# A six-stage transformer kernel: the scan's layer norm partly on ScalarE, one feed-forward norm inside the scan, three other seams reordered

## The reference

```python
x = x + _L0_xattn_ref(_layernorm(x), ctx_1024, ctx_1024, mask, ...)   # 16 heads, masked
x = x + _L0_attn_ref(_layernorm(x), L0_attn_context, ...)             # 8 heads of 128, shared context
x = x + _L0_ffn_ref(_layernorm(x), ...)                               # six attention nodes ("cell")
x = x + _L1_xattn_ref(_layernorm(x), ctx_1024)                        # no weights
x = x + _L1_attn_ref(_layernorm(x), ...)                              # linear scan over the sequence
x = x + _L1_ffn_ref(_layernorm(x), ...)                               # 256 -> 1024 -> 256, gelu
```

## Time and profile before

| | us |
|---|---|
| three runs | 2956.18, 2957.56, 2959.49 (median 2957.56) |
| profiled execution, its own time | 2957.78 |
| span of that execution, first to last instruction | 2955.8 |
| PE busy | 2823.1 (96%) |
| DVE busy | 2156.6 (73%) |
| ACT busy | 2036.0 (69%) |
| POOL busy | 1177.1 (40%) |

### The profile page before, as it was taken

How to read it: one execution, slowest core, us unless ns; L and a number is a source line. 1 busy time by engine, 2 the same in 40 slices (tenths; PEclk the granted TensorE clock), 3 DMA queues, 4 the chain that set the end, 5 groups by cost and what they waited for, 6 DMA issues and landing times. The chain is left out here.

```text
span 2955.8 us, 84436 instructions
## 1 busy us (share of the span) xinstructions
PE 2823.1 (96%) x31996; PEld 2198.5 (74%) x31996; DVE 2156.6 (73%) x5328; ACT 2036.0 (69%) x4128; POOL 1177.1 (40%) x962
## 2 busy tenths in 40 slices
PE   7999999799999999999989999999999999889999
PEld 6888888556666666666677887887888788556798
DVE  7888888777777767777736787787777777678443
ACT  6888888787777777777706766776667777333444
POOL 6777777576665656666600011011011100121310
PEclk9999999999999999999999999999999999999999
DMA  4111111077777887787851112111111103450000
GB/s 152 52 60 50 62 50 50 9 139 147 154 160 155 166 161 163 162 174 154 194 193 63 38 45 73 38 42 46 52 45 46 48 31 137 161 191 1 8 22 29
DMA packets 613611, 275.10 MB, mean 93 GB/s; under 512 B 548763, under 2 KB 589654, under 8 KB 613094
## 3 DMA queue, kind: packets, MB, share of 16 engines
q1 hardware_dynamic: 597958, 231.16, 32.6%
q10 hardware_dynamic: 15360, 39.85, 3.8%
HBM read 119.40 MB, written 17.30 MB: 46 GB/s over the span
## 5 line engine op out<-in xcount | busy, mean ns | idle before, releaser
L1645 POOL TENSOR_TENSOR front_parts<-front_prob,front_parts 128x1024 f16<-128x1024 f32 x256 | 545.6, 2132 | 328.0 <-ACT front_parts L1853 294.4
L1943 DVE TENSOR_REDUCE wide_row_max<-wide_score 128x1 f32<-128x1024 f32 x256 | 312.5, 1221 | 125.9 <-PE wide_score L1686 125.5
L1841 ACT ACTIVATE front_prob<-wide_score,wide_neg_max,front_s_up 128x1024 f32<-128x1024 f32 x256 | 307.7, 1202 | 123.8 <-DVE wide_neg_max L1946 118.7
L1686 PE MATMUL wide_score<-wide_kT,wide_qT 128*128 128x512 f16 x1536 | 375.6, 381 | 6.2 <-ACT front_prob L1841 4.6
L2248 POOL TENSOR_TENSOR cell_w<-cell_w_stage,cell_w 128x1536 fp32r<-128x1536 f32 x23 | 80.5, 3498 | 637.4 <-ACT cell_w L2519 637.4
L954 POOL TENSOR_TENSOR common_common<-common_common,mask_inv_sum 128x512 f32<-128x512 f32 x256 | 272.1, 1063 | 107.8 <-DVE mask_inv_sum L1352 105.2
L1209 ACT ACTIVATE common_common<-common_common,mask_row_min 128x256 f32<-128x256 f32 x512 | 254.8, 502 | 48.0 <-DVE mask_row_min L1300 47.7
L1853 ACT ACTIVATE front_parts<-front_prob 128x1024 f16<-128x1024 f32 x256 | 269.9, 1054 | 13.8 <-ACT front_prob L1841 7.0
L1686 PEld LDWEIGHTS wide_score<-wide_kT,wide_qT 128*128 128x128 f16 x1536 | 144.5, 98 | 154.2 <-ACT front_prob L1841 6.9
L2708 DVE TENSOR_REDUCE cell_row_max<-cell_score 128x8 f32<-128x512 f32 x192 | 131.0, 682 | 152.8 <-PE cell_score L2349 151.0
L1300 DVE CUSTOM_DVE_ANT_0 common_common<-mask_score,front_prob 128x256 f32<-128x256 f32 x512 | 189.1, 417 | 3.5 <-issue 3.5
(11 more groups left out here) (349 smaller groups left out, 6591.6 us busy)
## 6 DMA issues: line engine op xcount, KB each, us to landing
cell_w_stage<-cell_weights ACTq DMA_DIRECT2D x24, 768.0 KB, 5.1
front_cT<-in_ctx_turned SPq DMA_DIRECT2D x32, 512.0 KB, 3.3
ahead_home<-in_ctx_odd SPq DMA_DIRECT2D x16, 1024.0 KB, 5.6
cell_w_stage<-in_L_ffn_W_own ACTq DMA_DIRECT2D x24, 512.0 KB, 3.6
front_prob<-in_mask_BxS_ik SPq DMA_DIRECT2D x32, 256.0 KB, 3.5
front_probT<-front_parts SPq DMA_TRANSPOSE x512, 2.8
ahead_home<-in_ctx_even SPq DMA_DIRECT2D x16, 512.0 KB, 4.0
common_common<-in_L_ffn_W_pairs SPq DMA_DIRECT2D x10, 512.0 KB, 4.3
```

The lines of the kernel that those rows point to most:

```text
L1645: pool.tensor_tensor(parts[:, s % 2, LO, :], prob[:, s % 2, :], parts[:, s % 2, HI, :], ALU.subtract).then_inc(part_lo, 1)
L1686: mm = pe.matmul(score[:, s % 2, half * 512:(half + 1) * 512], qT[:, u_par, a, s * P:(s + 1) * P], kT[:, par, b, half * 512:(half + 1) * 5 ...
L1841: act.activation(prob[:, s % 2, :], score[:, s % 2, :], ACT.Exp, bias=neg_max[:, s % 2:s % 2 + 1], scale=s_up[:, 0:1], accum_out=row_sum[: ...
L1943: dve.tensor_reduce(row_max[:, one], score[:, s % 2, :], AX.X, ALU.max).then_inc(max_found, 1)
```

## The change

It has five parts.

1. Scan: the apply of blocks 3 to 7 moves from VectorE (the end of step n) to ScalarE, behind `gate_of(n + 2)`. GpSimd computes the shift, with two small instructions for each block.
2. Feed-forward norm of block 0: stats and apply on VectorE in step 6 of the scan, around the straight-through of the second weight; its transposes in step 7, ahead of the second weight's; its copies there too. The two `keep_clock` calls go.
3. The low-rank products, merges and splits of the second weight move from the end of the scan into the first `fc` of the feed-forward, one to each of its eight steps.
4. Masked attention: unit 0's rows are the first DMA. Cell: in the last step block 6's stats and apply come ahead of the low half, its scale and add behind it, with the norms of context units 0 and 1 between them; GpSimd's order follows.
5. Feed-forward: the last block is stored in two halves.

```diff
+    def gpsimd_shift(self, pool, n):
+        at = n - self.first_shift + 1
+        pool.tensor_scalar(self.neg_mean[:, :], self.mean_var[:, :, 0], -1.0, None, ALU.mult).then_inc(self.negated, 1)
+        pool.wait_ge(self.negated, at)
+        pool.wait_ge(self.rstd_ready, n + 1)
+        pool.tensor_tensor(self.shift[:, :], self.neg_mean[:, :], self.rstd[:, :], ALU.mult).then_inc(self.shift_ready, 1)
+
+    def scalar_apply(self, act, n, x):
+
+        act.wait_ge(self.turned, n * DH)
+        act.wait_ge(self.shift_ready, n - self.first_shift + 1)
+        for s in range(SUB):
+            ins = act.activation(self.xn[:, s, :], x[:, s, :], ACT.Identity, bias=self.shift[:, s:s + 1], scale=self.rstd[:, s:s + 1])
+        ins.then_inc(self.xn_ready, 1)
...
+    def tensor_low_rank_late(self, pe, banks, t):
+        out, lhsT, rhs, _ = self.products[self.fc_loras + t]
+        if t == 0:
+            pe.wait_ge(self.prep_copied, len(self.turns))
+        if t >= 2:
+            pe.wait_ge(self.weights_ready, self.fc_loras + t - 1)
+        pe.matmul(banks[t % 2][:, 0:rhs.shape[1]], lhsT, rhs, start=True, stop=True).then_inc(self.lora_ready, 1)
...
@@ masked attention, SP @@
+        load_rows(0, 0)
         sp.dma_start(wT[:, :, :, :], W_turned).then_inc(w_loaded, 16)
...
@@ cell, POOL and DVE @@
+            for X in range(1 if last else 2):
+                last_norm.gpsimd_rstd(pool, i * 2 + X)
             if last:
                 for k in range(2):
                     ahead.gpsimd_rstd(pool, k, k)
-            for X in range(1 if last else 2):
-                last_norm.gpsimd_rstd(pool, i * 2 + X)
...
                 if final and X == 1:
-                    for k in range(2):
-                        ahead.vector_stats(dve, k, k)
-                        ahead.vector_apply(dve, k, k)
+                    finish_stats(i, 0, last)
+                    ahead.vector_stats(dve, 0, 0)
+                    ahead.vector_finish_norm(dve, i * 2)
+                    ahead.vector_apply(dve, 0, 0)
                 for hf in range(DH):
...
                 if final and X == 1:
-                    finish(i, 0, last)
+                    ahead.vector_finish_scale(dve, i * 2)
+                    ahead.vector_finish_add(dve, i * 2, 0)
+                    ahead.vector_stats(dve, 1, 1)
+                    ahead.vector_apply(dve, 1, 1)
...
@@ scan, POOL @@
         for n in range(1, NBLK):
+            if n >= FIRST_SHIFT:
+                pool.wait_ge(norm.xn_ready, n)
             norm.gpsimd_rstd(pool, n)
-        ffn.gpsimd_lo(pool, 0, ffn.loras)
+            if n >= FIRST_SHIFT:
+                norm.gpsimd_shift(pool, n)
+        ffn.norm.gpsimd_rstd(pool, 0)
+        ffn.gpsimd_lo(pool, 0, ffn.fc_loras)
...
@@ scan, PE @@
             if n == 7:
+                ffn.norm.tensor_turn(pe, 0, False)
                 ffn.tensor_turn(pe, ffn_banks, ffn.fc_turns, len(ffn.turns))
...
-        ffn.tensor_low_rank(pe, ffn_banks, ffn.fc_loras, ffn.loras)
...
@@ scan, ACT @@
             if follows(n, 2):
                 copy_hi(n + 2)
                 gate_of(n + 2, False)
+            if follows(n, 3):
+                norm.scalar_apply(act, n + 3, of_block(n + 3))
...
             if n == 7:
+                ffn.scalar_turned_hi(act, turn_banks, 0)
                 ffn.scalar_copy(act, ffn_banks, ffn.fc_turns, len(ffn.turns))
-                ffn.scalar_hi(act, ffn.fc_loras, ffn.loras)
...
@@ scan, DVE @@
             if n == 6:
+                ffn.norm.vector_stats(dve, 0, of_block(0))
                 ffn.vector_straight_through(dve, 1)
+                ffn.norm.vector_apply(dve, 0, of_block(0), False)
+            if n == 7:
+                ffn.vector_turned_lo(dve, turn_banks, 0)
             finish(n)
...
-            if n == 7:
-                ffn.vector_merge(dve, ffn_banks, ffn.fc_loras, ffn.loras)
-            if follows(n, 3):
-                norm.vector_apply(dve, n + 3, of_block(n + 3), True)
...
@@ feed-forward, PE @@
-        keep_clock(pe, const["ident"], out_banks[1], 32)
-        norm.tensor_turn(pe, 0, False)
-        keep_clock(pe, const["ident"], out_banks[1], 24)
...
                 mm.then_inc(fc_ready, 1)
+                if first:
+                    ffn.tensor_low_rank_late(pe, out_banks, t)
 
         def project(n, j, first, last):
+            if first:
+                pe.wait_ge(ffn.weights_ready, ffn.loras)
...
@@ feed-forward, ACT (gelu) and DVE (split_hidden) @@
+                if first:
+                    ffn.scalar_hi(act, ffn.fc_loras + t, ffn.fc_loras + t + 1)
...
             for t in range(FT):
+                if first:
+                    ffn.vector_merge_late(dve, out_banks, t)
                 dve.wait_ge(gelu_done, n * FT + t + 1)
```

More of the change, by code:

```diff
@@ L148, in vector_apply, with add_shift @@
         ins.then_inc(self.xn_ready, 1)
+    def add_shift(self, mem, name, first):
+        self.first_shift = first
+        self.neg_mean = mem.sb(name + "neg_mean", [P, SUB])
+        self.shift = mem.sb(name + "shift", [P, SUB])
+        self.negated = mem.sem(name + "negated")
+        self.shift_ready = mem.sem(name + "shift_ready")
+    def gpsimd_shift(self, pool, n):
[10 more added lines that the diff above has]
+        ins.then_inc(self.xn_ready, 1)
     def tensor_turn(self, pe, n, has_last):
@@ L215, in __init__ @@
         self.inv_scale = mem.sb("inv_scale", [P, 2])
+        self.norm = BlockNorm(mem, const, True, name="ffn_")
+        self.xnT = mem.sb("ffn_xnT", [P, 2, DH, BLK], F32R)
+        self.xn_hi = mem.sem("xn_hi")
         self.w_split = {"fc": mem.sb("ws_fc", [P, 2, DH, F], F32R), "proj": mem.sb("ws_proj", [P, 2, FT, D], F32R)}
@@ L363, in tensor_low_rank, with vector_merge_late, scalar_turned_hi, vector_turned_lo @@
             pe.matmul(bank[:, 0:rhs.shape[1]], lhsT, rhs, start=True, stop=True).then_inc(self.lora_ready, 1)
+    def tensor_low_rank_late(self, pe, banks, t):
[5 more added lines that the diff above has]
+        pe.matmul(banks[t % 2][:, 0:rhs.shape[1]], lhsT, rhs, start=True, stop=True).then_inc(self.lora_ready, 1)
+    def vector_merge_late(self, dve, banks, t):
+        n = self.fc_loras + t
+        out = self.products[n][0]
+        dve.wait_ge(self.lora_ready, n + 1)
+        dve.scalar_tensor_tensor(out, banks[t % 2][:, 0:out.shape[1]], self.LORA, out, ALU.mult, ALU.add).then_inc(self.weights_ready, 1)
+    def scalar_turned_hi(self, act, banks, n):
+        for h in range(DH):
+            act.wait_ge(self.norm.turned, n * DH + h + 1)
+            act.activation(self.xnT[:, self.HI, h, :], banks[h][:, :], ACT.Copy).then_inc(self.xn_hi, 1)
+    def vector_turned_lo(self, dve, banks, n):
+        for h in range(DH):
+            dve.wait_ge(self.xn_hi, n * DH + h + 1)
+            dve.tensor_tensor(self.xnT[:, self.LO, h, :], banks[h][:, :], self.xnT[:, self.HI, h, :].bitcast(F32), ALU.subtract)\
+                .then_inc(self.norm.turn_copied, 1)
     def vector_merge(self, dve, banks, first, end):
@@ L893, in _, with load_rows @@
     def _(sp):
+        def load_rows(u, k):
+            sp.dma_start(x_of(u), x_in[rows(u * P, P), :]).then_inc(x_loaded[k], 16)
+        load_rows(0, 0)
         sp.dma_start(wT[:, :, :, :], W_turned).then_inc(w_loaded, 16)
@@ L900, in load @@
                 sp.wait_ge(in_turned, u - 1)
-            sp.dma_start(x_of(u), x_in[rows(u * P, P), :]).then_inc(x_loaded[k], 16)
+            if not isinstance(u, int) or u > 0:
+                load_rows(u, k)
             if later(u):
@@ L3108, in stage_scan @@
     norm.banks = turn_banks
+    FIRST_SHIFT = 3
+    norm.add_shift(mem, "norm_", FIRST_SHIFT)
+    ffn.norm.banks = turn_banks
     wo, wc, wb, wt, rows2 = front.wo, front.wc, front.wb, front.wt, front.rows2
@@ L3321, in stats_of @@
         def stats_of(n):
+            if n > FIRST_SHIFT:
+                dve.wait_ge(norm.shift_ready, n - FIRST_SHIFT)
             norm.vector_stats(dve, n, of_block(n))
@@ L3427, in add_bias @@
             pool.tensor_tensor(of_block(n), of_block(n), ffn.out_bias[:, :].unsqueeze(1).to_broadcast([P, SUB, D]), ALU.add).then_inc(bias_added, 1)
-        norm.gpsimd_rstd(pool, 0)
+        norm.gpsimd_rstd(pool, 1)
+        ffn.gpsimd_lo(pool, ffn.fc_loras, ffn.loras)
         add_bias(0)
-        with pool.Fori(1, NBLK) as n:
+        add_bias(1)
+        with pool.Fori(2, NBLK) as n:
             norm.gpsimd_rstd(pool, n)
@@ L3444, in fc @@
             if first:
[L3445 removed]
+                pe.wait_ge(ffn.w_lo, ffn.fc_loras)
             for t in range(FT):
@@ L3480, in _ @@
     def _(act):
-        def turned_hi(n):
-            for h in range(DH):
-                act.wait_ge(norm.turned, n * DH + h + 1)
-                act.activation(xnT[:, HI, h, :], turn_banks[h][:, :], ACT.Copy).then_inc(xn_hi, 1)
         def gelu(n, j, first, last):
@@ L3530, in low @@
             return dve.tensor_tensor(dst, src, hi.bitcast(F32), ALU.subtract)
-        def turned_lo(n):
```

(5 more changed lines are left out.)

36 lines of the change are left out of this document (21 added, 15 removed).

## The result

The changed kernel took 2984.48 us (median of 4 runs, 2974.07 to 2992.84), the kernel before 2958.52 beside it (4 runs, 2956.18 to 2961.91). The ratio is 1.0079, 95% interval 1.0061 to 1.0097: slower by 26 us, 17.5 above the top of the predicted range.

A forecast was written before the change was run, and what follows sets the result against it. TensorE, busy 96% of the span, was taken as the bound, with more to win in the seams than in the scan. Terms of -2.4 - 3.7 - 0.9 - 0.4 + 4.0 - 0.8 + 4.4 = +0.2 gave 2958.0 us, range 2949 to 2967.

The forecast's parts named there:

- Start and end of the cell: Kernel's start, unit 0's rows issued first: -2.4 us; cell's end, ScalarE's last copy no longer waiting for VectorE: -3.7.
- clock of the seam: Behind the cell, less TensorE idle time may keep its clock up: -0.9 us, between 0 and -1.8.
- store: Kernel's end, only 256 KB left to store behind the last add: -0.8 us, between 0 and -1.5.
- Gaps of the scan: Scan, TensorE waits for ScalarE's apply behind the gate, four gaps of 3.45 us: +11.1.
- Steps 4 to 7: Late scan, a later ScalarE copy, block 0's stats and apply, and eight transposes lengthen the path: +5.95 us.
- Seam to the feed-forward: Scan's last add to first `fc`, only barrier and start remain, 0.9 us in place of 18.3: -17.4.
- First `fc`: First feed-forward block, eight low-rank products between groups and a late last merge: +4.0 us, bounds 2.5 and 6.
- The clock in the scan: Scan, TensorE's clock may fall in four gaps, 1.1 us each, between 0 and 2.2: +4.4.
- Rival C: Scan, the clock falls at each boundary and stays low: 2964.9 us, 2970 at 4 a gap; chance 0.22.
- Rival B: Scan, the moved apply stays hidden, TensorE's gap remaining near 0.65 us: 2941 us; chance 0.07.

The follow-up runs named there:

- e4: The kernel before with only unit 0's rows first, the cell's last norm reordered and the last store in two halves: 2950.13 us, ratio 0.9966.
- e1: The changed kernel with 32 identity transposes put back ahead of the first `fc`: 2970.78 us, ratio 1.0055.
- e9: The changed kernel with one edit, ScalarE's apply in the scan ahead of the gate instead of behind it: 2948.28 us, ratio 0.9954.
- e8: The changed kernel with the apply ahead of the gate and the low-rank products two each behind `fc` groups 4 to 7: 2938.97 us, ratio 0.9935.
- e7: The changed kernel with the low-rank products two each behind groups 4 to 7 of the first `fc`, scan untouched: 2983.36 us, ratio 1.0075.
- e11: The kernel before with only the apply of blocks 3 to 7 moved to ScalarE, behind the gate: 2995.36 us, ratio 1.0112.
- e10: The changed kernel with 28 identity transposes starting scan steps 1 to 4, and low-rank products behind `fc` groups 4 to 7: 2956.85 us, ratio 0.9991.
- e3: The changed kernel with 32 identity transposes ahead of the first `fc` and ScalarE's apply ahead of the gate: 2942.24 us, ratio 0.9949.
- e12: The kernel before with only the apply of blocks 3 to 7 moved to ScalarE, ahead of the gate: 2955.17 us, ratio 0.9986.
- e2: The changed kernel with the second weight's low-rank products, merges and splits back at the scan's end, no transposes: 2967.64 us, ratio 1.0036.

## Why the prediction was wrong

The sum was made of terms, most of them right.

- Start and end of the cell, -2.4 and -3.7, clock of the seam -0.9, store -0.8: right, and e4 measured -8.9 for all four. The start gave more than its term: the wide attention's first transposes stand at 563.5 on average in the eleven profiles with the new start and at 566.8 in the three without, 3.3 earlier. PE's idle time behind the cell fell from 5.36 to 1.71. The scan starts 6.34 earlier in the profile, but the cell with that idle time took 1031.6 to 1038.2 us among those eleven, so one profile can't weigh this.
- Gaps of the scan, +11.1: right in mechanism and size (13.6 in four waits, less the 2.6 of before).
- Steps 4 to 7, +5.95: it was 7.2, and the clock makes the difference. From the scan's first transposes to the end of its last product PE takes 25.1 us longer (124.4 against 99.3). Of these 1.0 lie ahead of the first gap, where the clock was lower (0.50 in the first 2.7 us, transposes of 1.94 in place of 1.06), and 16.9 in the four steps, 11.0 as gaps and 5.8 as clock. Behind them 7.2 are left. The wait for the small transposes is as forecast: 2.37 in place of 0.41 and 1.06, +0.9 for +0.95. But the clock fell in it as well, and the step behind it is 1.5 longer. The wait for the merges grew by 2.5, of which VectorE's own wait of 0.93 for GpSimd's rstd, ahead of block 0's apply, is a part that the term doesn't have.
- Seam to the feed-forward, -17.4: right (1.0 us from the end of the last add to the first `fc`, 17.3 less).
- First `fc`, +4.0 (2.5 to 6): at full clock it is +6.2 (e1: 8 x 2.21 against 11.46). A product took 0.62 from start to start, not 0.43, and a group 1.59 in place of 1.41. This term was mis-sized from three products that were timed back to back. Its +0.6 for the last merge is not seen: `project` follows the transposes at once.
- Not in the sum, nor among the rivals: the clock in the first `fc`, +8.8 in the profile, 5.6 by e9 against e8. The prediction put it at nothing without a reason. Its one row on this seam is in the earlier trace rows, 2.5 us idle with the clock kept. Behind that gap stood plain `fc` groups, and ahead of it 32 + 24 transposes. The change took the transposes away and put 16-row products between the groups.
- **The clock in the scan, +4.4 (0 to 2.2 a gap): the step that failed.** The upper end came from one low spell of 4.4 busy microseconds. It assumed that a fallen clock comes back soon. In the profiled run it did (5.8 for the four gaps), but e7 and e11 show whole steps at 1.2 GHz, 5.4 more each. e10 against e7 puts the clock's share at 25 us, and e9 against the changed kernel at some 23. So the term was too small by some 20 us. With 20 more, 5.6 to 8.8 for the first `fc`'s clock and 2.2 for its size the forecast of 2958.0 would be 2986 to 2989, against 2984.5 measured; that is an estimate from differences between kernels, each with its noise. The earlier trace rows had also shown the clock lost at 2.0 us, so the length of a gap did not sort its own rows. Rival C had the right mechanism and the wrong price: 2964.9 at 2.6 a gap, 2970 at 4.
- Rival B was set aside with "the order of the three instructions, which I see no way around". That was right for this change, and a swap of two calls (e3, e9, e12) was the way around.

The Trainium skill's rule on idle gaps, weighed in the prediction, would have paid each gap in full, and that was the better guide: the clock fell at all four. At the prediction's 2.2 us a gap that is 8.8, still too low. The page ("TensorE: Matmul & The Clock Gate", "What's actually happening") also says, of a kernel's start, that the number of matmuls run at the low clock differs between runs of one kernel. The traces agree, in the middle of a kernel: four runs of the changed kernel had mean clocks of 0.972 to 0.981 and lay 19 us apart. A row is one such run, and its price is a sample.

## What to carry to other kernels

When work moves to another engine, put it in that engine's order where its inputs are ready, not at the end of the step: on the kernel before, the same four instructions cost 36 us behind the gate and gained 4 ahead of it. Price a new idle gap on TensorE by the worst case of what follows it, a full step or block at half the clock, not by one spell of the old trace. And look at what stands between a seam and dense work before removing it: the kernel before had transposes that compute nothing ahead of its first `fc`, and that `fc` ran at full clock; where they must go, products of 128 rows first and the small ones late is the order of the fastest kernel here (e8, 2938.97, 0.65% below the kernel before), though its gain over e9 is within the noise.

## What was not expected of the hardware

A busy TensorE is no proof of a full clock. In the changed kernel's first `fc` PE was busy without a break from 2767 to 2784 at a granted clock of 0.50, while it ran groups of six 128-row matmuls with two 16-row ones between. In e9 it was 19 us, from 2749 to 2768. Identity transposes in front (e1), plain groups (e2) and plain groups first (e8: 8.70 us for five) brought it back to full, in e1 within the 32 transposes. The scan's steps alternate 128-row and 17-row products too, and there e11's clock was at 0.50 in nearly all the work of three steps in a row, the last with 2.0 us of idle time ahead of it. The Trainium skill ("TensorE: Matmul & The Clock Gate", "What's actually happening") says that activity is what releases the clock. These rows don't contradict it, but they show work that kept the engine busy and did not. The same mix did not pull a full clock down in e1, over 17.6 us. That the small products are why a fallen clock stayed low fits these runs and was not tried by itself.

Whether the clock falls at a given gap also varied. At 1.72 us idle it fell, then or within two groups, in the changed kernel, e8 and e9, and did not in e7 and e10, whose five plain groups took 7.07 and 7.08 us. At 1.57 us idle e1's 32 transposes took 5.04 us, and e3's 3.68. At 2.37 us the changed kernel's next eight transposes took 1.91, and e10's 1.04.
